# One core, attention then experts: new orders, shifts on VectorE, decayed keys as one product on GpSimd

## What is computed

```python
def layernorm(x): return (x - mean(x)) / sqrt(var(x) + 1e-5)
# block 1: attention with a decaying state, 4 heads of 64 columns, on n = layernorm(x)
#   v = n @ W_write.T, keys = n shifted by one row, queries = n
#   reads[t] = alpha * sum over s < t of gamma**(t-1-s) * (n[t] . n[s-1]) * v[s], per head
x = x + (n + reads @ W_read.T)
# block 2: 8 experts, the best 2 of each row, on m = layernorm(x)
probs = softmax(m @ gate_w.T); top2 = top_k(probs, 2)
# each row m:
x = x + sum over its 2 experts of prob * (gelu(m @ w1[e] + b1[e]) @ w2[e] + b2[e])
```

## Time and profile before

| | us |
|---|---|
| median of 3 runs | 571.51 |
| lowest and highest | 568.94, 571.64 |
| span of the profiled execution | 576.6 |
| TensorE busy in it | 534.6 |
| VectorE busy | 457.3 |
| ScalarE busy | 332.8 |
| GpSimd busy | 244.5 |

### The profile page before, as it was taken

One profiled execution on the slowest core, in us unless ns is written; L12 is line 12 of the kernel. 1 busy time (PEld: TensorE's weight loads), 2 busy tenths in 40 slices (PEclk: granted clock), 3 DMA queues, 4 the chain that ended last, 5 costly groups with the idle time before them and its releaser, 6 DMA issues.

```text
span 576.6 us, 17660 instructions
## 1 busy us (share of the span) xinstructions
PE 534.6 (93%) x5246; PEld 418.7 (73%) x5246; DVE 457.3 (79%) x1408; ACT 332.8 (58%) x841; POOL 244.5 (42%) x275
## 2 busy tenths in 40 slices
PE   7799889899988888999999999999999999999991
PEld 7677777777776656777777777777777777777770
DVE  5889999999976789777887877777777887877771
ACT  5899989888744633444545444544454545444540
POOL 2426778888846532432333222333332333222333
PEclk8999999999998979999999999999999999999996
DMA  5577767667334353444444344444444433444432
GB/s 162 199 221 224 254 205 214 188 216 215 122 96 123 113 179 58 78 71 68 67 65 62 63 70 75 78 75 75 70 71 67 68 62 62 65 69 76 76 48 27
DMA packets 85097, 63.34 MB, mean 110 GB/s; under 512 B 54224, under 2 KB 77392, under 8 KB 85008
## 3 DMA queue, kind: packets, MB, share of 16 engines
q1 hardware_dynamic: 71328, 43.94, 31.0%
q0 software_dynamic: 13392, 18.27, 17.1%
q10 hardware_dynamic: 288, 0.00, 0.0%
HBM read 37.56 MB, written 24.62 MB: 108 GB/s over the span
## 4 chain that ended last, share of the span: by engine, by line
PE 63%; DVE 13%; POOL 8%; issue 8%; ACT 3%; SPq 1%; DMA 1%; another core or an unknown queue 0%; ACTq 0%; DVEq 0%; POOLq 0%
PE psum L1518 29%; PE psum L1533 20%; PE psum L1535 10%; POOL sent_rows L501 4%; DVE weights L779 2%; POOL tiny L491 2%; POOL tiny L488 1%; DVE arena L915 1%; SPq L429 1%; PE psum L1338 1%; DVE tiny L858 1%; DMA arena<-in_x 1%; DVE tiny L881 1%; DVE arena L1146 1%; DVE arena L851 1%
## 5 line engine op out<-in xcount | busy, mean ns | idle before, releaser
L1518 PE MATMUL psum<-arena,weights 128*128 128x256 f16 (+1 forms) x2208 | 281.4, 250 | 4.3 <-issue 4.3
L1518 PEld LDWEIGHTS psum<-arena,weights 128*128 x2208 | 188.8, 99 | 83.1 <-issue 6.6
L737 ACT ACTIVATE arena<-psum,b_cur 128x256 f32<-128x256 f32 (+1 forms) x368 | 131.7, 423 | 159.9 <-PE psum L1518 120.4
L532 POOL DMA_INDIRECT out<-arena,tile_in x71 | 115.0, 1620 | 251.6 <-DVE arena L1161 150.3
L1533 PE MATMUL psum<-weights,arena 128*128 x568 | 215.7, 381 | 2.1 <-DVE arena L1148 2.1
L1535 PE MATMUL psum<-weights,arena 128*128 x568 | 155.4, 274 | 0.0
L1148 DVE TENSOR_TENSOR arena<-arena 128x512 f16<-128x512 f32 x142 | 99.6, 701 | 4.9
L501 POOL DMA_INDIRECT sent_rows<-arena,tiny x64 | 65.3, 1021 | 27.3 <-issue 16.6
L1146 DVE CAST arena<-arena 128x512 f16<-128x512 f32 x142 | 61.8, 435 | 6.1 <-ACT arena L737 5.8
L1533 PEld LDWEIGHTS psum<-weights,arena 128*128 128x128 f16 x568 | 55.8, 98 | 8.7 <-issue 2.6
L1535 PEld LDWEIGHTS psum<-weights,arena 128*128 128x128 f16 x568 | 55.8, 98 | 4.8
(11 more groups left out here) (172 smaller groups left out, 641.8 us busy)
## 6 DMA issues: line engine op xcount, KB each, us to landing
weights<-in_experts SPq DMA_DIRECT2D x32, 512.0 KB
arena<-sent_rows SPq DMA_DIRECT2D x100, 64.0 KB
arena<-in_b SPq DMA_DIRECT2D x46, 128.0 KB
arena<-in_x SPq DMA_DIRECT2D x16, 256.0 KB, 3.7
out<-arena SPq DMA_DIRECT2D x16, 256.0 KB, 4.1
arena<-sent_rows SPq DMA_DIRECT2D x84, 32.0 KB
sent_rows<-pad SPq DMA_DIRECT2D x7, 265.0 KB
tile_in<-sent_rows SPq DMA_DIRECT2D x71, 4.5 KB
```

What stands on the lines that cost most here:

```text
L532: pool.indirect_dma_start(out=out, out_offset=bass.IndirectOffsetOnAxis(ap=at_u, axis=0), in_=yout[:, u % 4], in_offset=None, compute_op=A ...
L737: last = a.activation(act[:, g % 2, m * n:(m + 1) * n], ps_h[:, g % 2, m * n:(m + 1) * n], ACT.Gelu_apprx_tanh, scale=1.0 / WSCALE, bias=b ...
L1518: last = pe.matmul(ps_h[:, f % 2, mm * n:(mm + 1) * n], w1_of(e_of[i], k, lo, per * (f - GROUP[i]) + mm), turned[:, i % 2, part, k, 0:n], ...
```

## The change

The keys' product moves to GpSimd, where it is one instruction in the step behind the two powers and ahead of the scatters. GpSimd no longer makes the shifts; VectorE makes each in one instruction (chunk_shift and residual_shift), so it waits for GpSimd's power. The first moments get a second buffer. The orders of the steps change on ScalarE, VectorE and TensorE, and one weight piece moves from step 7 to step 2.

```diff
-PIECES = (0, 0, 1, 3, 3, 3, 3, 3, 2, 2, 2, 2, 2, 2, 2, 2)
+PIECES = (0, 0, 2, 3, 3, 3, 3, 2, 2, 2, 2, 2, 2, 2, 2, 2)
...
-        moments1 = by_batch(small(B * 2))
+        moments1 = [by_batch(small(B * 2)) for _ in range(2)]
...
+            def chunk_keys(m):
+
+                s = m % 2
+                reached(pool, "xn_done", m)
+                if m == 0:
+                    pool.wait_ge(setup_act, 3)
+                reached(pool, "state_ps", m - 2)
+                by_head = lambda t: t[:, s].rearrange("p b (h d) -> p b h d", h=H)
+                pool.tensor_tensor(by_head(keys), by_head(xn),
+                                   decayK[:].unsqueeze(1).unsqueeze(3).to_broadcast([P, B, H, HD]),
+                                   ALU.mult).then_inc(S["keys_done"], 1)
...
                         reached(pool, used, m - ago - 1)
-                        pool.tensor_scalar(ve, moments[:, :, 1], EPS, None, ALU.add)
-                        pool.tensor_scalar(shift, moments[:, :, 0], -1.0, None, ALU.mult).then_inc(S[mid], 1)
+                        reached(pool, end, m - 1)
+                        pool.tensor_scalar(ve, moments[:, :, 1], EPS, None, ALU.add).then_inc(S[mid], 1)
                         reached(pool, mid, m)
                         pool.tensor_tensor(rs, ve, minus_half[:].to_broadcast([P, B]), ALU.pow).then_inc(S[end], 1)
-                        reached(pool, end, m)
-                        pool.tensor_tensor(shift, shift, rs, ALU.mult).then_inc(S[last], 1)
+                if 1 <= n < NCH:
+                    chunk_keys(n - 1)
                 if active(n, 5):
```

On ScalarE chunk_keys is gone, and the step is now:

```diff
                 if 1 < n <= NCH + 1:
                     last_column(n - 1)
+                if active(n, 4):
+                    normed_transposed(n - 4)
                 if active(n, 1):
                     chunk_high(n - 1)
                 for j in splits(n)[0:1]:
                     split_high(j)
-                if active(n, 1):
-                    chunk_residual(n - 1)
                 if active(n, 5):
                     exponential(n - 5)
-                if 1 <= n < NCH:
-                    chunk_keys(n - 1)
-                for j in splits(n)[1:2] if len(splits(n)) > 2 else ():
+                for j in splits(n)[1:-1]:
                     split_high(j)
                 if active(n, 2):
                     chunk_values(n - 2)
-                if active(n, 4):
-                    normed_transposed(n - 4)
-                for j in splits(n)[2:] if len(splits(n)) > 2 else splits(n)[1:]:
-                    split_high(j)
+                if active(n, 1):
+                    chunk_residual(n - 1)
                 if active(n, 0):
                     chunk_normalise(n)
+                for j in splits(n)[1:][-1:]:
+                    split_high(j)
```

VectorE (carry and choose move back, split_low of all but the last two pieces stands where one stood, the last two at the end of the step):

```diff
+            def chunk_shift(n):
+
+                reached(v, "rs1_done", n)
+                v.scalar_tensor_tensor(out=shift1[n % 2], in0=moments1[n % 2][:, :, 0], scalar=-1.0, in1=rs1[n % 2],
+                                       op0=ALU.mult, op1=ALU.mult).then_inc(S["shift1_done"], 1)
...
-                if active(n, 3):
-                    carry(n - 3)
                 if active(n, 0):
                     moments(n)
-                if active(n, 5):
-                    choose(n - 5)
                 if active(n, 1):
                     chunk_low(n - 1)
...
+                if active(n, 3):
+                    carry(n - 3)
                 if active(n, 1):
                     chunk_queries(n - 1)
                 if active(n, 3):
                     residual(n - 3)
-                for j in splits(n)[0:1]:
+                if active(n, 5):
+                    choose(n - 5)
+                for j in splits(n)[:-2]:
                     split_low(j)
                 if active(n, 3):
                     residual_stats(n - 3)
+                if active(n, 0):
+                    chunk_shift(n)
                 if active(n, 5):
                     weigh_gates(n - 5)
...
                 if active(n, 4):
                     logits(n - 4)
+                if active(n, 3):
+                    residual_shift(n - 3)
...
-                for j in splits(n)[1:]:
+                for j in splits(n)[-2:]:
                     split_low(j)
```

In the opening VectorE's chunk_shift(0), (1) and (2) stand ahead of first_normalise(0), first_normalise(1) and mask_decay, and ScalarE splits two pieces of step 2. TensorE:

```diff
+                if active(n, 4):
+                    turn_normed(n - 4)
                 if active(n, 3):
                     project(n - 3)
-                if active(n, 4):
-                    turn_normed(n - 4)
...
+                if active(n, 4):
+                    score_experts(n - 4)
                 if 2 <= n <= NCH:
                     states(n - 2)
-                if active(n, 4):
-                    score_experts(n - 4)
```

More of the change, by code:

```diff
@@ L210, in build @@
         small_at = [0]
-        tiny = sb("tiny", [P, 188])
+        tiny = sb("tiny", [P, 192])
         def small(w, dt=F32):
@@ L234, in build @@
         slots = by_batch(small(B * E))
-        assert small_at[0] <= 188
+        assert small_at[0] <= 192
         pick = sb("pick", [P, B, 2, E])
@@ L473, in _ @@
             pool.wait_ge(setup_pool, 1)
+            def chunk_keys(m):
[8 more added lines that the diff above has]
+                                   ALU.mult).then_inc(S["keys_done"], 1)
             def step(n):
                 par = n % 2
[L478 to L482, removed]
+                for lag, moments, ve, rs, got, mid, end, used, ago in (
+                        (0, moments1[par], ve1, rs1[par], "moments1_done", "ve1_done", "rs1_done", "res_done", 1),
+                        (3, moments2, ve2, rs2, "moments2_done", "ve2_done", "rs2_done", "xm_done", 0)):
                     if active(n, lag):
@@ L603, in normalise @@
                 last.then_inc(S["xm_done"], 1)
[L605 to L614, removed]
             def chunk_values(m):
@@ L714, in _ @@
             decay_table()
-            chunk_keys(0)
             chunk_values(0)
             chunk_normalise(2)
-            chunk_keys(1)
-            split_high(0)
+            for j in splits(2):
+                split_high(j)
             reads_high(0)
@@ L786, in moments @@
                 reached(v, "stats1_done", n)
-                reached(v, "ve1_done", n - 1)
+                reached(v, "ve1_done", n - 2)
                 for b in range(B):
-                    last = v.bn_aggr(moments1[:, b], stats1[:, b])
+                    last = v.bn_aggr(moments1[n % 2][:, b], stats1[:, b])
                 last.then_inc(S["moments1_done"], 1)
+            def chunk_shift(n):
+                reached(v, "rs1_done", n)
+                v.scalar_tensor_tensor(out=shift1[n % 2], in0=moments1[n % 2][:, :, 0], scalar=-1.0, in1=rs1[n % 2],
+                                       op0=ALU.mult, op1=ALU.mult).then_inc(S["shift1_done"], 1)
             def largest(m):
@@ L867, in residual_moments, with residual_shift @@
                 last.then_inc(S["moments2_done"], 1)
+            def residual_shift(m):
+                reached(v, "rs2_done", m)
+                v.scalar_tensor_tensor(out=shift2, in0=moments2[:, :, 0], scalar=-1.0, in1=rs2, op0=ALU.mult,
+                                       op1=ALU.mult).then_inc(S["shift2_done"], 1)
             def logits(m):
@@ L1239, in _ @@
             moments(1)
+            chunk_shift(0)
             first_normalise(0)
@@ L1242, in _ @@
             first_residual(0)
+            chunk_shift(1)
             first_normalise(1)
@@ L1252, in _ @@
             chunk_queries(0)
+            chunk_shift(2)
             mask_decay()
@@ L1268, in _ @@
             split(0)
+            residual_shift(NCH - 1)
             place(m)
```

## The result

The kernel after takes 578.50 us (median, 577.03 to 581.79), the kernel before in the same runs 570.23: ratio 1.0158, 95% interval 1.0109 to 1.0208. It is slower, and near the forecast of 579.6.

The account below looks back on a forecast made before the run. VectorE was taken to bound three-piece steps, POOL most two-piece steps. Step terms +7.7, opening +1.0 and step 16 -0.6 gave +8.1 us on the 571.5 median: 579.6; range 566 to 584, the forecast's own 576 to 584.

Parts of the forecast that it names:

- the hold: Attention steps: VectorE, reaching picked (both inputs in SBUF) during the keys' product on GpSimd, waits until it ends; 1.0 us a step.
- Product on GpSimd, 1.1 us: Keys' product over 128x512 on GpSimd, behind the second power: 1.1 us, taken as two passes.
- 1.2 + 1.1 - 1.37: Hold per step: product starts 1.2 us after L866 ends, takes 1.1; VectorE reaches picked at 1.37; 0.9, 1.0 with hand-over.
- 11.6 and 10.5: Forecast lengths in us of attention steps with three weight pieces (11.6) and with two (10.5).
- Step 3, +1.2: Attention step starting at 22.30 us in the first trace of before: forecast to take 1.2 us more.
- step 7, 10.5: Attention step that loses a weight piece and becomes a two-piece step: forecast 10.5 us, +0.1 against before.
- The base: Time before the change: two-piece steps 10 to 13 at 10.30 to 10.36 us; span difference carried to the 571.5 median.
- Opening +1.0: Opening: keys of chunk 1 meet mask_decay, chunk_shift(2) waits about 0.6 us, the piece fills idle time; 0 to 2, taken +1.0.
- step 16 -0.6: Step 16: TensorE's 0.66 us wait for ScalarE goes, as in the steps before; -0.6 us.
- Shifts, +0.2 a step and no wait: VectorE gains two products on two columns, +0.2 us a step; residual_shift's wait for the power costs nothing.
- rival 1: Keys' product short, 0.6 to 0.8 us, or hold partial, 0.5 a step: +1.6, 573 us; chance 0.08.
- Rival 3: Nothing is held: two-piece steps cost 9.5 us, sum -5.1, time 566.4 us; chance 0.27.

Follow-up runs that it names:

- memsets: Kernel after with the keys' product on GpSimd replaced by two memsets (416 and 512 columns), keys zero: 576.55 us, ratio 1.0148.
- new trace of before: Kernel before, unchanged, run and traced a second time: 569.07 us against 569.27, ratio 1.0005, span 566.8.
- 4-column kernel: Kernel after with the keys' product over 4 of 64 columns per head, keys zeroed once in the opening: 573.65 us, ratio 1.0077.
- last group: Last group of runs, in which the unchanged kernel before took 578.71 us; the kernel before with the product alone on GpSimd took 584.67, ratio 1.0125.

## Why the prediction was right, and where it was not

The total came out (579.6 against 578.5) and the main mechanism, the hold, too. But three terms were mis-sized, 3.7 us too much and some 6 too little, and offset each other in part; that the total is this near is partly luck.

- **Product on GpSimd, 1.1 us** (bounds 0.63 and 1.5): measured 1.04 in all 15. Two passes was the right pick. The Trainium skill's 2.6 cycles per element (GPSIMD Engine Reference, section 3.1), for which I had estimated about 1.1, agrees within 6%.
- **VectorE is held, as the later one**: right, at picked as forecast. The memsets show that it takes more than a GpSimd instruction that writes SBUF. In steps 3 and 4 residual_shift is the one that is held.
- **Size of the hold, 1.0 a step**: mis-sized. It is 0.60 on picked and 0.48 on the step. The rows give 116.15 + 1.04 - 116.46 = 0.73 from picked's start to the product's end, where I had 1.2 + 1.1 - 1.37 and 0.07 of hand-over. The product starts 0.1 earlier than I had it, and picked's own 0.18, which it needs in any case, I had counted as loss. Over steps 5, 6 and 8 to 14 this made the forecast 3.7 us too large: 11.6 and 10.5, measured 11.16 and 10.09.
- **Step 3, +1.2, and step 7, 10.5**: too small. They took 12.15 (+3.4 on the new trace of before) and 11.17. I looked for VectorE's own work in the opening and not at who waits behind it. The chain is chunk_shift(2), mask_decay, weigh_scores, 3.38 us of idle TensorE, reads at the lower clock level, and a late transposed chunk for which VectorE waits 2.2 in step 3. To this comes the hold of residual_shift, 0.84. Step 7 shows the chain again on a smaller scale, in the timelines of TensorE and VectorE:

```profile
64.99 1.47 PE L1422 MATMUL psum<-arena 128*64 128x128 f32 x16 [1.51 <-DVE arena L908]
66.39 1.97 PE L1429 MATMUL psum<-arena 64*64 64x128 f32 x16
...
68.30 0.96 PE L1376 MATMUL psum<-consts,arena 128*128 128x128 f32 x4
```

```profile
70.86 0.69 DVE L892 TENSOR_TENSOR arena<-psum,arena 128x512 f16<-128x512 f32 x1 [1.03 <-ACT arena L637]
```

 TensorE idles 1.51, its next reads take 1.97 at the lower clock level, the transposed chunk reaches ScalarE late and VectorE waits 1.03. The 4-column kernel has the same in its early steps, so most of it does not need the full product. Nor does it need the new orders: step 3 takes 11.32 with the shifts alone and 11.21 with shifts, product and old orders, but 9.27 with the product alone. By one trace of each, the start of step 8 comes at 72.50 in before, 74.90 with the shifts alone and 78.07 in the 4-column kernel: 2.4 us go with the shifts, 3.2 with the new orders, the moved piece and the small product. The one exception is the kernel with the keys back on ScalarE, whose step 3 takes 9.62 with shifts and new orders.
- **The base**: the 10.3 us of steps 10 to 13 in the earlier trace rows were those of one long execution; 9.75 is usual. With that the same step values would have summed to 3 us more (0.55 in each of steps 10 to 13 and 15, 0.3 in step 9), and the forecast would have been near 583. The span stood 5.1 above the median, and I said so but carried every difference over unchanged. That was the choice that went wrong, and luck that it offset the hold.
- **Opening +1.0, step 16 -0.6**: step 3 starts 1.2 later than in the old trace; from step 15 to the end after needs 0.4 less than the new trace of before. Both hold, though it was chunk_shift(2) and not mask_decay that the keys of chunk 1 met.
- **Shifts, +0.2 a step and no wait**: there is no wait in after (L776 and L859 in two-piece steps), because the new order places chunk_shift late enough; with the old order it waits 0.3. VectorE's order is what brings two-piece steps from 10.38 to 10.09, and I had not priced it. The size is nearer 0.3: 9.61 without the hold, against the 9.30 of step 8 before.
- **Rivals**: partial hold (rival 1, given 0.08) is nearest to what the steps did, though its price of 573 missed the early steps. Rival 3, nothing held, would have shown 9.5: the 4-column kernel does just this (9.61) and still loses 0.8%, so it too was priced wrong. Its gain needed steps of 10.3 before, which the second trace of before doesn't have.

What remains open: why the time from step 15 on is 8 us longer in the last group and 7 in the first trace of before; why the 4-column kernel's execution times spread so wide (570.0 to 578.8) and the memset kernel lies above it; what lengthens single scatters of GpSimd; and the separate share of ScalarE's and TensorE's new orders, which no run isolates.

## What to carry to other kernels

Before moving elementwise work to GpSimd, look at what VectorE runs in that time: a VectorE instruction with both inputs in SBUF that starts while such a product runs waits for its end, be it small (picked, 0.78 instead of 0.18) or large (two split_lows, 3.10 instead of 2.35), so a 1 us product can take 0.6 us from an engine that doesn't run it. A power on two columns held nothing. Ask of each moved instruction who waits behind it, in the opening as well, since an idle TensorE can pay twice, by the wait and by its clock afterwards. And before a difference is taken from one trace, check its span against the median of the times: where they differ by 1%, as here, a loop of the trace may have run at another period than it usually does.

## What the runs showed of the hardware that I had not expected

- The hold works in both directions: an epsilon addition and a shift product of GpSimd on two columns take 1.23 and 1.14 instead of 0.22 and 0.20 beside a split of VectorE, and VectorE's picked 0.78 instead of 0.18 beside a product of GpSimd. Memsets of 416 and 512 columns on GpSimd don't hold it (0.18), though it overlaps both.
- A VectorE instruction on two columns can be held as long as a large one: chunk_shift(2), 0.99 instead of 0.15.
- The loop of the kernel before has more than one period with one program: two-piece steps of 9.3, 9.75 or 10.3, and the length of GpSimd's instructions that end with a split of VectorE differs with it (1.23 or 0.67).
- After 3.38 and 1.51 us without work TensorE's reads took up to 1.97 us instead of 1.09; after 1.75 us in another run, and after 2.78 us in the kernel with shifts, product and old orders, they took 1.09. The length of the idle time alone doesn't settle it.
